# Graph network with layer norm on one core: the inverse deviations of the first four row blocks by Newton steps on GpSimd, and their early normalization

## The chip, the cores and the metric

One core of one Trainium2 chip runs the whole kernel. The metric is device time in microseconds (us). The kernel before has a median of 664.06 us over 3 runs (664.0 to 664.29).

## The reference, cut to what matters

The inputs are a node matrix x (2048 x 256) and an adjacency matrix adj (2048 x 2048, int32). Five steps of a gated graph network change a state that begins as x. Then an output head, a residual and a layer norm follow; the change is in that last part.

```python
state = x
for _ in range(5):
    a = concat([A @ (state @ in_W.T + in_b), A.T @ (state @ out_W.T + out_b), state])
    r = sigmoid(a @ r_W.T + r_b); z = sigmoid(a @ z_W.T + z_b)
    h_hat = tanh(concat([a_in, a_out, r * state]) @ h_W.T + h_b)
    state = (1 - z) * state + z * h_hat
hid = tanh(state @ o1_W.T + o1_b)
v = x + hid @ o2_W.T + o2_b
out = (v - mean(v)) / sqrt(var(v) + 1e-5)      # over the 256 columns of each row
```

## The kernel before, in words

Each engine has one instruction stream, written out by hand in program order, and semaphores order the streams among each other. An engine never passes a waiting instruction of its own, so the order of the source is the order of the work. (`general_path`, for a matrix that isn't symmetric, doesn't run here.)

The 2048 rows are 16 blocks of 128 rows (NB = 16), and 4 blocks make a chunk (BC = 4, NC = 4). The network's steps hold the state transposed (`stateT`, 128 partitions x 2 halves x 2048 columns), and every product is made of three matmuls of high and low parts: an operand is copied to its high part by ACT (`high`, L811) and its low part is a subtraction on DVE (`low`, L1136). The steps fill the span up to about 638 us. The change is in what follows them.

The stages at the end, for each chunk c:

- `update_last` (DVE, L1582): the last change of the state of chunk 3, six operations on 128x512 values at L1588, L1591, L1593 and L1595, behind the last gate at L1280.
- `final_split` (ACT `final_high`, DVE `low`): the high and low parts of the final state.
- `hidden` (TensorE, then ACT L1001 `hidden_tanh` and L1007 `hidden_high`): the hidden layer, its tanh and its high part. `split_hidden` (DVE, L1542) makes the low part. One of the eight low parts, half 1 of chunk 2, is made on GpSimd at L534.
- `output` (TensorE, L763): 24 matmuls of 256 columns; after each two blocks it signals `o_done`.
- `residual`, `moments`, `aggregated` (DVE, L1548 to L1566): adds x to two blocks (tile `a` of the profile, `y` in the code), takes the statistics of each block, and folds them to mean and variance (`mv`).
- `deviation` (ACT, L1109): sqrt(var + eps) for a batch of blocks. `inverse` (DVE, L1568): the reciprocal `rstd`, and `shift` = -mean * rstd.
- `normalize`: on ACT (L1115, a scaled Identity with the shift as bias), on DVE (L1578) for the blocks in `BY_DVE` = 12, 14, 15, and on GpSimd (L537) for `BY_POOL` = 2, 5, 10.
- The stores (SyncE, L454): blocks 0 to 3, 4 to 7, 8 to 11, 12 to 13, 14 to 15, in this order; each waits for the counts of blocks that ACT, DVE and GpSimd have normalized.

ACT's table of functions is changed once in this part: sqrt comes after the last tanh (the first sqrt, L1107, is there to make the load early). So the four deviation batches, (0 to 7), (8 to 11), (12, 13), (14, 15), all lie behind the last tanh, and chunk 0, whose variances are ready some 12 us earlier, waits with them. After the steps, GpSimd's stream holds only L534 and the three normalizations. Ahead of the last part DVE's stream (L1622 on) reads

```python
update_last(LAST, NC - 1)
final_split(3)
split_hidden(2)
residual(1, 0)
moments(1, 0)
```

and goes on with chunks 1 to 3 and the four `inverse` batches between them. ACT's stream there is: both `hidden_tanh(2, e)`; `final_high(3, e)` and `hidden_high(2, e)` in turn; `hidden(3)`; the table's load; the deviations and normalizations.

Of the kernel before, what the change touches and what calls it, by code (L numbers as in the profile page):

```python
# [11 lines left out]

# [1 line left out]

# [5 lines left out]
I32 = mybir.dt.int32  # L22
# [3 lines left out]
ALU = mybir.AluOpType  # L26
ACT = mybir.ActivationFunctionType

P = 128
CW = 512  # L30
EPS = 1e-5
# [10 lines left out]
def fast_path(nc, block, flag, flag_ready, y_stored, x, adj, in_W, in_b, out_W, out_b, r_W, r_b, z_W, z_b, h_W, h_b,  # L42
              o1_W, o1_b, o2_W, o2_b, out):
    N, D = x.shape
    NB, NC, DB = N // P, N // CW, D // P
    BC = CW // P
# [49 lines left out]
    with ExitStack() as ctx:  # L96
        def sb(name, shape, dt=F32):
            return ctx.enter_context(nc.sbuf_tensor(name, shape, dt))

        def sem(name):  # L100
            return ctx.enter_context(nc.semaphore(name))
# [31 lines left out]
        std = sb("std", [P, NB])  # L133
        rstd = sb("rstd", [P, NB])
        shift = sb("shift", [P, NB])
        above = sb("above", [P, NC * NP])
        differ = sb("differ", [P, 2 * NC])
        odd = sb("odd", [P, 3])
# [154 lines left out]
        hid_hi = sem("f_hid_hi")  # L293
        hid_lo = sem("f_hid_lo")
        hid_lo_pool = sem("f_hid_lo_pool")
        o_read_pool = sem("f_o_read_pool")
        o_done = sem("f_o_done")
        o_read = sem("f_o_read")
        xr_loaded = sem("f_xr_loaded")
# [33 lines left out]
        x_v = x.rearrange("(b p) d -> p b d", p=P)  # L333
        adj_v = adj.rearrange("(j p) i -> p j i", p=P)

        BATCHES = [(0, NB - 2 * BC), (NB - 2 * BC, NB - BC), (NB - BC, NB - 2), (NB - 2, NB)]
        BY_DVE = [NB - 4, NB - 2, NB - 1]
        BY_POOL = [2, 5, 10]

        starts = [c * BC for c in range(NC)] + [NB - 2, NB]  # L340

# [121 lines left out]
        def _(pool):  # L463
# [64 lines left out]
            pool.wait_ge(row_lo, row_count(1, (NC - 1, 1)))  # L528
            sum_blocks(1, range(6))

            c, e = 2, 1
            pool.wait_ge(fin_lo, NC * DB)
            pool.wait_ge(hid_hi, c * DB + e + 1)
            nc.gpsimd.tensor_tensor(hid_c[c % 2][LO][:, e, :], stateT[:, e, c * CW:(c + 1) * CW],  # L534
                                    hid_c[c % 2][HI][:, e, :].bitcast(F32), ALU.subtract).then_inc(hid_lo_pool, 1)

            for m in BY_POOL:  # L537

                pool.wait_ge(shift_ready, 1 + (m >= BATCHES[0][1]))
                nc.gpsimd.tensor_scalar(y[:, m, :], y[:, m, :], mv[:, m, 0:1], rstd[:, m:m + 1],  # L540
                                        ALU.subtract, ALU.mult).then_inc(y_pool, 1)

        @block.tensor
# [264 lines left out]
        def _(act):  # L809
# [197 lines left out]
            def hidden_high(c, e):  # L1007

                act.wait_ge(hid_act, c * DB + e + 1)

                wait(act, o_done, (c - 1) * (BC // 2))
                high(hid_c[c % 2][HI][:, e, :], stateT[:, e, c * CW:(c + 1) * CW], hid_hi)

            def hidden(c):

                for e in range(DB):
                    hidden_tanh(c, e)
                for e in range(DB):
                    hidden_high(c, e)
# [82 lines left out]
            for e in range(DB):  # L1102
                final_high(3, e)
                hidden_high(2, e)
            hidden(3)

            nc.scalar.activation(std[:, 0:1], ones[:, 0:1], ACT.Sqrt).then_inc(std_first, 1)  # L1107
            act.wait_ge(std_first, 1)
            def deviation(n):  # L1109

# [10 lines left out]
                                             bias=shift[:, m:m + 1]).then_inc(y_act, 1)  # L1121

            deviation(0)
            normalize(0, 0, BC + 1)
            deviation(1)
            normalize(0, BC + 1, 2 * BC)
            deviation(2)
            normalize(1, 2 * BC, 3 * BC)
            deviation(3)
            normalize(2, 3 * BC, 3 * BC + 2)  # L1130

        @block.vector
        def _(dve):
# [433 lines left out]
            def inverse(n):  # L1568

                a, b = BATCHES[n]  # L1570
                dve.wait_ge(std_ready, n + 1)
                nc.vector.reciprocal(rstd[:, a:b], std[:, a:b]).then_inc(rstd_ready, 1)
                dve.wait_ge(rstd_ready, n + 1)
                if n < len(BATCHES) - 1:
                    nc.vector.scalar_tensor_tensor(out=shift[:, a:b], in0=mv[:, a:b, 0], scalar=-1.0, in1=rstd[:, a:b],
                                                   op0=ALU.mult, op1=ALU.mult).then_inc(shift_ready, 1)

            def normalize(m):  # L1578
                nc.vector.tensor_scalar(y[:, m, :], y[:, m, :], mv[:, m, 0:1], rstd[:, m:m + 1],
# [59 lines left out]
            moments(3, 1)  # L1639
            inverse(2)  # L1640
            aggregated(3, 2, BC)
            normalize(BY_DVE[0])
            inverse(3)
            normalize(BY_DVE[1])
            normalize(BY_DVE[2])

    return len(starts) - 1

# [393 lines left out]
```

## Time and profile before

| what | value |
|---|---|
| median of 3 runs | 664.06 us |
| time of the profiled execution | 664.53 us |
| its span | 662.7 us |
| TensorE busy | 650.3 us, 98% |
| VectorE busy | 516.4 us, 78% |
| ScalarE busy | 348.5 us, 53% |
| GpSimd busy | 51.9 us, 8% |

The span is what the profiler records of the profiled execution; the 1.8 us by which its time is longer lie around it. PE is TensorE's matmul side, DVE VectorE, ACT ScalarE, POOL GpSimd, SP SyncE with its queue of DMAs. A line of the timeline gives start and duration in us, the engine, the source line, the operation, the tile written and the tiles read, the shapes and the count of instructions that were merged; a square bracket gives the idle time of the engine before it and who ended it. Two instructions of one engine that follow each other overlap a little, so the start-to-start distance is less than the duration.

### The profile page before, as it was taken

How to read it: one execution, taken by the hardware profiler on the slowest of the kernel's cores; microseconds unless marked ns; L12 is line 12 of the kernel's file. 1: busy time of each engine (PE TensorE's matmuls, PEld its weight loads, DVE VectorE, ACT ScalarE, POOL GpSimd, SP SyncE). 2: the span in 40 equal slices, each digit the busy share in tenths (PEclk: the TensorE clock that was granted, in tenths of full speed). 3: DMA queues.
4: the chain of work that ended last, by engine and by line, in shares of the span. 5: the costliest groups of instructions: out<-in, count | busy, mean ns of one | idle time of the engine just before them, and what ended most of it. 6: DMA issues, size and time to landing. Idle time of an engine off the chain costs nothing.

```text
span 662.7 us, 8577 instructions
## 1 busy us (share of the span) xinstructions
PE 650.3 (98%) x2940; PEld 539.6 (81%) x2940; DVE 516.4 (78%) x838; ACT 348.5 (53%) x486; POOL 51.9 (8%) x49
## 2 busy tenths in 40 slices
PE   8999999999999999999999999999999999999993
PEld 7888888888888888888888888888888888888883
DVE  4976878699687969967796997687789858855886
ACT  2873735477156337724562683366057525724646
POOL 0074034200500000000000000000000000000002
PEclk9999999999999999999999999999999999999998
DMA  8996533213000130300003022000322200013003
GB/s 293 305 405 242 169 130 107 42 42 54 2 0 32 50 47 33 50 14 0 32 33 62 0 63 32 0 32 32 52 44 60 35 1 1 0 64 127 1 2 130
DMA packets 90515, 46.72 MB, mean 70 GB/s; under 512 B 72176, under 2 KB 78960, under 8 KB 90224
## 3 DMA queue, kind: packets, MB, share of 16 engines
q1 hardware_dynamic: 86128, 45.77, 23.9%
q10 hardware_dynamic: 4352, 0.53, 0.5%
q8 instruction: 17, 0.28, 0.2%
q14 instruction: 18, 0.15, 0.1%
HBM read 32.12 MB, written 11.53 MB: 66 GB/s over the span
## 4 chain that ended last, share of the span: by engine, by line
PE 93%; DVE 2%; SPq 2%; DMA 2%; ACT 1%; issue 0%; DVEq 0%
PE bank L561 26%; PE bank L548 17%; PE bank L550 17%; PE bank L549 17%; PE bank L612 15%; DMA stage<-in_adj_dram 2%; SPq L393 1%; DVE stats L1560 1%; DVE a L1553 0%; DVE ring L1136 0%; SPq L389 0%; ACT a L1120 0%; DVE work L1593 0%; SPq L391 0%; DVE work L1588 0%
## 5 line engine op out<-in xcount | busy, mean ns | idle before, releaser
L561 PE MATMUL bank<-ring,rows 128*128 128x512 f32 x768 | 178.8, 389 | 0.3 <-ACT stateT L1091 0.3
L561 PEld LDWEIGHTS bank<-ring,rows 128*128 128x128 f32 x768 | 144.0, 188 | 30.6 <-ACT stateT L1091 0.5
L901 ACT ACTIVATE work<-work,bias 128x512 f32<-128x512 f32 x120 | 86.2, 723 | 155.5 <-DVE work L1280 154.9
L1280 DVE SCALAR_TENSOR_TENSOR work<-degree,deg_w,bank 128x512 f32<-128x512 uint16 x120 | 88.7, 745 | 57.5 <-PE bank L550 56.5
L548 PE MATMUL bank<-u_c,fold 128*128 128x512 f32 x240 | 93.5, 389 | 0.0
L550 PE MATMUL bank<-u_c,fold 128*128 128x512 f32 x240 | 93.4, 389 | 0.0
L549 PE MATMUL bank<-u_c,fold 128*128 128x512 f32 x240 | 93.4, 389 | 0.0
L612 PE MATMUL bank<-ring,rows 128*128 128x512 f32 x256 | 65.1, 391 | 0.0
L548 PE MATMUL bank<-st_c,own 128*128 128x512 f32 x160 | 62.3, 389 | 0.0
L550 PE MATMUL bank<-st_c,own 128*128 128x512 f32 x160 | 62.2, 389 | 0.0
L549 PE MATMUL bank<-st_c,own 128*128 128x512 f32 x160 | 62.2, 389 | 0.0
L833 ACT ACTIVATE ring<-sums,minus 128x1024 fp32r<-128x1024 uint8 x48 | 54.9, 1143 | 11.9 <-PE bank L612 11.3
L612 PEld LDWEIGHTS bank<-ring,rows 128*128 128x128 f32 x256 | 47.6, 188 | 11.1 <-issue 0.9
L550 PEld LDWEIGHTS bank<-u_c,fold 128*128 128x128 f32 x240 | 45.1, 188 | 9.4
L548 PEld LDWEIGHTS bank<-u_c,fold 128*128 128x128 f32 x240 | 45.0, 188 | 9.3
L549 PEld LDWEIGHTS bank<-u_c,fold 128*128 128x128 f32 x240 | 45.0, 188 | 9.3
L811 ACT ACTIVATE ring<-a 128x1024 fp32r<-128x1024 uint8 (+1 forms) x51 | 51.0, 1046 | 0.0
L1147 DVE CAST ring<-a 128x1024 fp32r<-128x1024 uint8 x64 | 44.5, 712 | 3.2 <-PE bank L561 2.9
L612 PE MATMUL bank<-ring,t_flat 128*128 128x512 f32 x192 | 46.7, 392 | 0.0
L612 PEld LDWEIGHTS bank<-ring,t_flat 128*128 128x128 f32 x192 | 35.4, 188 | 8.6 <-issue 0.6
L811 ACT ACTIVATE u_c<-bank 128x512 fp32r<-128x512 f32 x16 | 9.4, 591 | 60.6 <-PE bank L561 60.6
L534 POOL TENSOR_TENSOR ring<-stateT,ring 128x512 fp32r<-128x512 f32 x1 | 1.7, 1681 | 467.1 <-DVE rows L1136 467.1
(148 smaller groups left out, 985.0 us busy)
## 6 DMA issues: line engine op xcount, KB each, us to landing
stage<-in_adj_dram SPq DMA_DIRECT2D x15, 512.0 KB, 8.8
sums<-in_adj_dram SPq DMA_DIRECT2D x13, 512.0 KB, 8.5
turned_dram<-work SPq DMA_DIRECT2D x12, 512.0 KB, 2.6
rows<-turned_dram SPq DMA_DIRECT2D x192, 32.0 KB, 2.0
work<-in_x_dram SPq DMA_DIRECT2D x4, 512.0 KB, 10.2
x_dram<-work SPq DMA_DIRECT2D x4, 512.0 KB, 8.9
a<-x_dram SPq DMA_DIRECT2D x4, 512.0 KB, 5.3
a<-in_adj_dram SPq DMA_DIRECT2D x3, 512.0 KB, 11.5
```

Of the source, the lines that this page charges most:

```text
L393: sp.dma_start(x_raw[:, c * BC:(c + 1) * BC, :], x_v[:, c * BC:(c + 1) * BC, :]).then_inc(x_loaded[c], 16)
L548: nc.tensor.matmul(out_, wh, vh, start=first, stop=False)
L549: nc.tensor.matmul(out_, wh, vl, start=False, stop=False)
L550: return nc.tensor.matmul(out_, wl, vh, start=False, stop=last)
L561: m = nc.tensor.matmul(u_bank[2 * (c % 2) + d][:, :], rows[:, part, j, d * P:(d + 1) * P], tile[:, jj, :], start=(first and jj == 0 and pa ...
L612: last = nc.tensor.matmul(u_bank[BANK[kind]][:, :], product_rows(kind, part, 2 * p + jj), tile[:, jj, :], start=(kind in (P1, P5, P6, P4, ...
L811: nc.scalar.activation(out_, in_, ACT.Copy).then_inc(s, 1)
L833: nc.scalar.activation(ring[:, n % RING].rearrange("p j w -> p (j w)"), sums[:, 1 - side, m, h * 2 * CW:(h + 1) * 2 * CW], ACT.Identity, b ...
L901: nc.scalar.activation(gates[:, g, e, :], gates[:, g, e, :], ACT.Tanh if g == H else ACT.Sigmoid, bias=bias[:, g, e:e + 1]).then_inc(gate_ ...
L1147: nc.vector.tensor_copy(ring[:, n % RING], a8[:, 2 * side + kind, 2 * p:2 * p + 2, :]).then_inc(std_cast, 1)
L1280: nc.vector.scalar_tensor_tensor(out=gates[:, g, e, :], in0=degree[:, c * CW:(c + 1) * CW], scalar=deg_w[:, g, e:e + 1], in1=g_bank[s % 3] ...
L1560: nc.vector.bn_stats(stats[:, n, :], y[:, n, :]).then_inc(stats_ready, 1)
```

## The change

Sixteen small instructions on GpSimd, each waiting for the one before through a semaphore (`newton`), compute `rstd` and `shift` of blocks 0 to 3 from `mv`: var + eps, a first guess by integer arithmetic on its bits, three Newton steps of four instructions each, and the product with the mean, negated. GpSimd then normalizes block 3, and only after it comes its low part at L534. ACT waits for the result after `hidden_high(2, 1)` and normalizes blocks 0, 1 and 2 there, ahead of `hidden(3)`. The store of blocks 0 to 3 keeps its place in the SyncE queue. The batches of ACT and DVE become (4 to 7), (8 to 11), (12, 13), (14, 15). DVE normalizes block 15 alone; blocks 12 and 14 go to ACT, and DVE computes a shift for the last batch too.

```diff
--- before.py
+++ after.py
@@ -12,6 +12,7 @@
 
 
 
+import itertools
 from contextlib import ExitStack
 
 import concourse.bass as bass
@@ -133,6 +134,8 @@
         std = sb("std", [P, NB])
         rstd = sb("rstd", [P, NB])
         shift = sb("shift", [P, NB])
+        spread = sb("spread", [P, BC])
+        guess = sb("guess", [P, BC])
         above = sb("above", [P, NC * NP])
         differ = sb("differ", [P, 2 * NC])
         odd = sb("odd", [P, 3])
@@ -293,7 +296,8 @@
         hid_hi = sem("f_hid_hi")
         hid_lo = sem("f_hid_lo")
         hid_lo_pool = sem("f_hid_lo_pool")
-        o_read_pool = sem("f_o_read_pool")
+        newton = sem("f_newton")
+        early_ready = sem("f_early_ready")
         o_done = sem("f_o_done")
         o_read = sem("f_o_read")
         xr_loaded = sem("f_xr_loaded")
@@ -333,9 +337,9 @@
         x_v = x.rearrange("(b p) d -> p b d", p=P)
         adj_v = adj.rearrange("(j p) i -> p j i", p=P)
 
-        BATCHES = [(0, NB - 2 * BC), (NB - 2 * BC, NB - BC), (NB - BC, NB - 2), (NB - 2, NB)]
-        BY_DVE = [NB - 4, NB - 2, NB - 1]
-        BY_POOL = [2, 5, 10]
+        BATCHES = [(BC, 2 * BC), (2 * BC, 3 * BC), (3 * BC, NB - 2), (NB - 2, NB)]
+        BY_DVE = [NB - 1]
+        BY_POOL = [BC - 1, BC + 1, 2 * BC + 2]
 
         starts = [c * BC for c in range(NC)] + [NB - 2, NB]
 
@@ -528,17 +532,51 @@
             pool.wait_ge(row_lo, row_count(1, (NC - 1, 1)))
             sum_blocks(1, range(6))
 
+            links = itertools.count(1)
+
+            def link(instruction):
+
+                n = next(links)
+                instruction.then_inc(newton, 1)
+                pool.wait_ge(newton, n)
+
+            def scaled(out_, in_, factor, added):
+                link(nc.gpsimd.tensor_scalar(out_, in_, factor, added, ALU.mult, ALU.add))
+
+            def times(out_, a, b):
+                link(nc.gpsimd.tensor_tensor(out_, a, b, ALU.mult))
+
+            pool.wait_ge(aggr_ready, BC)
+            root, half_way = rstd[:, 0:BC], shift[:, 0:BC]
+            scaled(spread[:, :], mv[:, 0:BC, 1], 1.0, EPS)
+            scaled(root.bitcast(I32), spread[:, :].bitcast(I32), -0.5, 1597463007.0)
+            for _ in range(3):
+                times(half_way, root, root)
+                times(guess[:, :], half_way, spread[:, :])
+                scaled(half_way, guess[:, :], -0.5, 1.5)
+                times(root, root, half_way)
+            times(half_way, mv[:, 0:BC, 0], root)
+            nc.gpsimd.tensor_scalar(half_way, half_way, -1.0, 0.0, ALU.mult, ALU.add).then_inc(early_ready, 1)
+
+            def normalized(m):
+
+                if m < BC:
+                    pool.wait_ge(early_ready, 1)
+                else:
+                    pool.wait_ge(shift_ready, 1 + (m >= BATCHES[0][1]))
+                nc.gpsimd.tensor_scalar(y[:, m, :], y[:, m, :], mv[:, m, 0:1], rstd[:, m:m + 1],
+                                        ALU.subtract, ALU.mult).then_inc(y_pool, 1)
+
+            normalized(BY_POOL[0])
+
             c, e = 2, 1
             pool.wait_ge(fin_lo, NC * DB)
             pool.wait_ge(hid_hi, c * DB + e + 1)
             nc.gpsimd.tensor_tensor(hid_c[c % 2][LO][:, e, :], stateT[:, e, c * CW:(c + 1) * CW],
                                     hid_c[c % 2][HI][:, e, :].bitcast(F32), ALU.subtract).then_inc(hid_lo_pool, 1)
 
-            for m in BY_POOL:
-
-                pool.wait_ge(shift_ready, 1 + (m >= BATCHES[0][1]))
-                nc.gpsimd.tensor_scalar(y[:, m, :], y[:, m, :], mv[:, m, 0:1], rstd[:, m:m + 1],
-                                        ALU.subtract, ALU.mult).then_inc(y_pool, 1)
+            for m in BY_POOL[1:]:
+                normalized(m)
 
 
         @block.tensor
@@ -1102,9 +1140,13 @@
             for e in range(DB):
                 final_high(3, e)
                 hidden_high(2, e)
+            act.wait_ge(early_ready, 1)
+            for m in range(BC - 1):
+                nc.scalar.activation(y[:, m, :], y[:, m, :], ACT.Identity, scale=rstd[:, m:m + 1],
+                                     bias=shift[:, m:m + 1]).then_inc(y_act, 1)
             hidden(3)
 
-            nc.scalar.activation(std[:, 0:1], ones[:, 0:1], ACT.Sqrt).then_inc(std_first, 1)
+            nc.scalar.activation(std[:, BC:BC + 1], ones[:, 0:1], ACT.Sqrt).then_inc(std_first, 1)
             act.wait_ge(std_first, 1)
             def deviation(n):
 
@@ -1121,13 +1163,15 @@
                                              bias=shift[:, m:m + 1]).then_inc(y_act, 1)
 
             deviation(0)
-            normalize(0, 0, BC + 1)
+            normalize(0, BC, 2 * BC)
             deviation(1)
-            normalize(0, BC + 1, 2 * BC)
+            normalize(1, 2 * BC, 2 * BC + 1)
             deviation(2)
-            normalize(1, 2 * BC, 3 * BC)
+            normalize(1, 2 * BC + 1, 3 * BC)
+            normalize(2, 3 * BC, 3 * BC + 1)
             deviation(3)
-            normalize(2, 3 * BC, 3 * BC + 2)
+            normalize(2, 3 * BC + 1, 3 * BC + 2)
+            normalize(3, 3 * BC + 2, NB)
 
 
         @block.vector
@@ -1571,9 +1615,8 @@
                 dve.wait_ge(std_ready, n + 1)
                 nc.vector.reciprocal(rstd[:, a:b], std[:, a:b]).then_inc(rstd_ready, 1)
                 dve.wait_ge(rstd_ready, n + 1)
-                if n < len(BATCHES) - 1:
-                    nc.vector.scalar_tensor_tensor(out=shift[:, a:b], in0=mv[:, a:b, 0], scalar=-1.0, in1=rstd[:, a:b],
-                                                   op0=ALU.mult, op1=ALU.mult).then_inc(shift_ready, 1)
+                nc.vector.scalar_tensor_tensor(out=shift[:, a:b], in0=mv[:, a:b, 0], scalar=-1.0, in1=rstd[:, a:b],
+                                               op0=ALU.mult, op1=ALU.mult).then_inc(shift_ready, 1)
 
             def normalize(m):
                 nc.vector.tensor_scalar(y[:, m, :], y[:, m, :], mv[:, m, 0:1], rstd[:, m:m + 1],
@@ -1639,10 +1682,8 @@
             moments(3, 1)
             inverse(2)
             aggregated(3, 2, BC)
+            inverse(3)
             normalize(BY_DVE[0])
-            inverse(3)
-            normalize(BY_DVE[1])
-            normalize(BY_DVE[2])
 
     return len(starts) - 1
 
```

## Rows read from the trace of the kernel before

**Rows 1.** The page: busy time of each engine, its share of the span, instructions

```profile
PE 650.3 (98%) x2940; PEld 539.6 (81%) x2940; DVE 516.4 (78%) x838; ACT 348.5 (53%) x486; POOL 51.9 (8%) x49
```

**Rows 2.** The chain of work that ended last, from 637 us: start, duration, what

```profile
648.84 0.68 DVE ring L1136
...
655.01 1.47 ACT a L1120 x3
```

**Rows 3.** Timeline of ACT from 643 us

```profile
643.83 0.62 ACT L811 ACTIVATE ring<-stateT 128x512 fp32r<-128x512 f32 x1
646.31 1.37 ACT L1004 ACTIVATE stateT<-bank,bias 128x512 f32<-128x512 f32 x2 [1.86 <-PE bank L550]
647.57 1.14 ACT L811 ACTIVATE ring<-stateT 128x512 fp32r<-128x512 f32 x2
...
651.26 2.08 ACT L1120 ACTIVATE a<-a,shift,rstd 128x256 f32<-128x256 f32 x4 [0.69 <-DVE shift L1575]
...
656.50 0.30 ACT L1113 ACTIVATE std<-mv,eps 128x2 f32<-128x2 f32 x1
```

**Rows 4.** Timeline of DVE from 638 us

```profile
638.01 0.38 DVE L1566 BATCH_NORM_AGGREGATE mv<-stats 128x2 f32<-128x6 f32 x4
...
639.31 0.69 DVE L1588 TENSOR_TENSOR work<-work,stateT 128x512 f32<-128x512 f32 x1
...
644.57 0.69 DVE L1136 TENSOR_TENSOR ring<-stateT,ring 128x512 fp32r<-128x512 f32 x1
...
649.44 0.69 DVE L1553 TENSOR_TENSOR a<-bank,a 128x512 f32<-128x512 f32 x1
...
652.81 0.66 DVE L1553 TENSOR_TENSOR a<-bank,a 128x512 f32<-128x512 f32 x1
...
654.36 0.16 DVE L1575 SCALAR_TENSOR_TENSOR shift<-mv,rstd 128x4 f32<-128x4 f32 x1
...
656.14 0.16 DVE L1575 SCALAR_TENSOR_TENSOR shift<-mv,rstd 128x2 f32<-128x2 f32 x1
```

**Rows 5.** Groups of POOL's instructions, shapes apart: busy, mean ns, idle before

```profile
L477 POOL TENSOR_TENSOR deg_sum<-a 128x1024 uint32<-128x1024 uint32 x4 | 10.4, 2590 | 28.5 <-DVE a L1199 27.5 <-ACT t_flat L811 1.0
...
L540 POOL TENSOR_SCALAR a<-a,mv,rstd 128x256 f32<-128x256 f32 x3 | 3.7, 1224 | 5.8 <-DVE shift L1575 5.8
L477 POOL TENSOR_TENSOR deg_sum<-deg_sum 128x256 uint32<-128x256 uint32 x4 | 3.3, 824 | 0.3
...
L477 POOL TENSOR_TENSOR deg_sum<-deg_sum 128x128 uint32<-128x128 uint32 x4 | 1.8, 462 | 0.3
```

**Rows 6.** Timelines of DVE and POOL near 170 us and at 101 us

```profile
170.80 1.53 DVE L1147 CAST ring<-a 128x1024 fp32r<-128x1024 uint8 x1
...
101.93 1.04 POOL L507 TENSOR_TENSOR sums<-a,byte_two 128x512 uint32<-128x512 uint32 x1
...
170.29 1.49 POOL L507 TENSOR_TENSOR sums<-a,byte_two 128x512 uint32<-128x512 uint32 x1
```

**Rows 7.** Groups of DVE's instructions, shapes apart

```profile
L1147 DVE CAST ring<-a 128x1024 fp32r<-128x1024 uint8 x64 | 44.5, 712 | 3.2 <-PE bank L561 2.9 <-PE bank L612 0.2
```

**Rows 8.** Timelines of POOL and PE from 644 us

```profile
644.73 1.68 POOL L534 TENSOR_TENSOR ring<-stateT,ring 128x512 fp32r<-128x512 f32 x1 [467.09 <-DVE rows L1136]
...
646.79 0.28 PE L548 MATMUL bank<-t_flat,ring 128*128 128x256 f32 x1
...
652.43 0.28 PE L550 MATMUL bank<-t_flat,ring 128*128 128x256 f32 x1
```

**Rows 9.** Timeline of SP: the third and the fifth store's issue

```profile
656.56 0.37 SPq L460 DMA_DIRECT2D out_dram<-a  x1
...
657.85 0.71 SPq L460 DMA_DIRECT2D out_dram<-a  x1
```

**Rows 10.** Stretches of 1 us: length, busy of each engine, clock, DMA share, GB/s

```profile
658.00:659.00 1.00, 0.00 (x0) 0.00 (x0) 0.00 (x0) 0.00 (x0) 0.00 (x0) 0.50 1.03 345
...
661.00:662.00 1.00, 0.00 (x0) 0.00 (x0) 0.00 (x0) 0.00 (x0) 0.00 (x0) 0.50 0.06 23
```

## The prediction

> **What bounds the kernel now.** The page comes first: TensorE is busy for 98% of the span and GpSimd for 8% [rows 1]. That share says little here, since the change touches only what follows the network's steps, so the chain of waits is next. From 638.6 us on it runs almost only over DVE (the last state update, then chunk after chunk of low parts, residuals and statistics), and only at the end over ACT's last normalizations [rows 2]. The reader should see one place in it: at 648.84 DVE starts the second low part of hidden chunk 3, and ACT's high parts of the same chunk ended at 647.57 + 1.14 = 648.71 [rows 2, 3]. ACT has no slack there. If it is late with them, DVE is late by as much, and so is all that follows. In front of the last tanh, by contrast, ACT is idle for 1.86 us, until TensorE brings the hidden layer at 646.31 [rows 3]. That hole is where the change puts three normalizations. Last the stores: the fifth is issued at 657.85 [rows 9], and data flow at 345 GB/s in the stretch from 658 and still at 23 in that from 661 [rows 10].
>
> **Part 1, the Newton chain.** It can start when chunk 0 is aggregated, 638.01 + 0.38 = 638.4 [rows 4], and GpSimd is idle until 644.73 [rows 8]. The price of a 4-element instruction is in no row. The nearest are 2590 ns for 1024 elements and 462 for 128: slope 2.4 ns an element, so 0.17 us for 4 [rows 5]. The linked levels of the byte sums have 0.3 us of idle time over four, 0.08 each [rows 5]. So 0.25 us a step, and 16 steps make 4.0: ready at 642.4, while ACT asks for it at 643.83 + 0.62 = 644.45 [rows 3]. Undisturbed, the chain is free.
>
> But it isn't undisturbed. Near 170 us, where both engines read SBUF, a DVE cast takes 1.53 us instead of its mean of 0.71 [rows 6, 7], and the GpSimd instruction beside it 1.49 where the same form takes 1.04 at 101.93, beside a DVE instruction that reads PSUM [rows 6]. The two take turns, instruction by instruction: the cast issued at 170.80 ends only 0.55 us after GpSimd's, which began at 170.29 and ended at 171.78. L534 shows the same against a subtraction with two SBUF inputs: 1.68 us, beginning 0.16 us after it [rows 4, 8]. From 639.31 to 645.26 DVE runs nine such two-input instructions, almost gapless [rows 4]. In the 0.9 us ahead of 639.31 four steps fit. After that a step that has just ended starts the next one behind a DVE instruction that is already running, so it is one step per DVE instruction: nine more. Three are left at 645.26, 0.75 us. DVE pays too: each turn of GpSimd holds it for 0.17 less the 0.1 by which its own instructions overlap, 9 x 0.07 = 0.6. Ready at 645.26 + 0.75 + 0.6 = 646.6, 2.2 us after ACT asks. The ends: 0.12 us a step gives 645.9; no turns at all 642.4; a dearer tensor_scalar is a rival below. I take 646.6, because it's the cost that the nearest rows carry over to a small instruction.
>
> The Trainium skill says the same more strictly and against this change: in "SBUF — State Buffer", section "Who interferes with whom", a DVE instruction with two SBUF inputs contends with a GpSimd one that reads SBUF, and whoever issues second blocks fully. By that rule a step of 4 elements waits for a whole DVE instruction as a long one does, and the case below in which small steps slip through is excluded; no row here shows a step so small.
>
> **Part 2, ACT's three early blocks.** Four normalizations take 2.08 us with 0.59 for one [rows 3], so 0.5 from start to start, 1.5 for three. At the undisturbed time they would end by 646.05 in the hole of 1.86. At 646.6 the hole is over: the last tanh starts at 646.6 + 1.5 = 648.1, not at 646.31, **+1.8 us**. The high parts, the low parts on DVE and the rest of DVE's list shift by that; DVE's own 0.6 is inside it, since DVE would wait at the low parts anyway. The table's load and the deviations shift along.
>
> **Part 3, what queues on GpSimd and SyncE.** L534 now comes behind the chain and block 3 (1.22 us [rows 5]): 647.9, done at 649.2, where before it ended at 646.41 [rows 8]. `output(2)`, at 646.79 before [rows 8], starts then; `output(2)` and `output(3)` are 48 matmuls from 646.79 to 652.43 [rows 8], 0.12 apart, so 2.9 us each and 1.45 for two blocks. The first half is ready at 650.7, and DVE wants it at 649.44 + 1.8 = 651.2 [rows 4]: covered, by 0.5 us. Without that cover it would cost what exceeds it. `output(3)` then starts at 652.1, its first half is ready at 653.6 for a residual due at 652.81 + 1.8 = 654.6 [rows 4]. The store of chunk 0 goes out near 648; SyncE has nothing else queued then.
>
> **Part 4, the last three microseconds.** DVE loses blocks 12 and 14 and gains a shift (0.16, as [rows 4]). ACT loses blocks 0, 1 and 3 there and gains 12 and 14. Relative to the shifted time, ACT can start block 8 only after the shift at 654.36 [rows 4], about 0.2 after that starts, 654.57; the deviation of (12, 13) follows, then 9, 11 until 656.35, so the third store goes out at 656.44 instead of 656.56 [rows 9]. Block 12 starts at 656.35 behind the shift at 656.14 [rows 4], the last deviation at 656.85 instead of 656.50 [rows 3], the last shift near 657.4, block 14 until 658.2: the fifth store is issued at 658.3, 0.4 us later than now [rows 9]. It doesn't matter: from the third store on there is 1 MB to move, at 345 GB/s [rows 10] 3.0 us, and the third store's issue sets when that starts. That gives -0.1. And the thin flow of 661 to 662 us [rows 10], a fifteenth of the full rate, as one lagging DMA engine of 16 would leave behind 2 MB of stores in a row, may be gone once 0.5 MB leaves early: up to another -1.0. Ends -0.1 and -1.1; I take **-0.6**, halfway, since the lag's cause is in no row.
>
> **The sum.** +1.8 - 0.6 = +1.2 us on the profiled execution's own 664.53 (its span is 662.7), 665.7; that execution lies 0.5 above the median of the three runs, 664.06, so **665.3** for the median, +0.18%. A measurement of this kernel can tell about 0.2% from no change, 1.33 us: 662.7 to 665.4. The forecast is a small loss just inside that bound.
>
> **The rivals.**
>
> A. *Small steps slip through.* The chain ends at 642.4 as it would alone, but block 3 then takes its 1.22 us [rows 5] in the middle of the state update and holds DVE, about 1.1 us. The hidden layer of chunk 3 comes 1.0 late (TensorE waits for the low part). +1.0 - 0.6: 664.5. For it: 4 elements are little; against it: instructions of every size in the trace take turns.
>
> B. *Nothing collides at all.* The chain and block 3 run in idle time, ACT fills its hole, and only the end changes: -0.6, 663.5, at best -1.1, 662.9. This is as fast as the idea can be, since the path over DVE stays as long; it is still no difference that can be measured. Against it: the 1.53 us cast [rows 6].
>
> C. *Slower: GpSimd's tensor_scalar is dear to start.* Block-sized it takes 1.224 us for 256 elements where the two-input form takes 0.824 [rows 5]. If all 0.4 of that is start, a small one costs 0.57, and the chain has six. Two steps fit ahead of 639.31, nine are at DVE's turns, four of them long (4 x 0.5 + 5 x 0.07 = 2.3 of delay to DVE), five are left at about 0.45. Ready at 645.3 + 2.3 + 2.2 = 649.8, the tanh at 651.3, +5.0; the low parts can't hide it: 668.5 with the end's -0.6. It decides from about 0.25 us a tensor_scalar, where the forecast passes 0.2%; halfway to it stands 666.9. The Trainium skill speaks against C: "GPSIMD Engine Reference", section "4.1 Engine selection", has one-input operations roughly at line rate and two-input ones about twice as slow. By that the six would be the cheap ones of the chain; the rows with 256 elements show it the other way round.
>
> D. *The fifth store decides.* If the third store's data are through early, the 0.4 us by which the last shift is later stays: +1.8 + 0.4, 666.3. Against it: 3 us of transfer begin before.
>
> **How the numbers follow.** Forecast 0.47 (its own range 664.1 to 666.1: a chain that ends from 645.9 to 646.9, and the end's -0.1 to -1.1), A 0.17, B 0.12, C 0.14 with its halfway, D 0.05, the rest is what I don't see. Slower by over 0.2%: somewhat less than half of the forecast's case (0.21), C, D: 0.41. Faster by over 0.2%: only beyond B's best, 0.07. Within: 0.52. The range goes from 663.2, between B's value and its best, to 667.2, past C's halfway, and leaves out C's full price.
>
> **What would show it.** In the profile after: the sixteen POOL rows from 638.4 on, at 0.25 us until 639.3 and then at about 0.65, DVE's rate; at 0.25 throughout, A or B is right; at 0.5 and more ahead of 639.3, C. ACT's first early block at 646.7 with idle time before it that GpSimd ends; the last tanh at 648.1; DVE waiting at the low parts of chunk 3 for about 1.2 us. Two-input DVE rows of 0.75 in place of 0.69. No lag behind the last megabyte where -1.1 is right. The forecast is wrong if the last tanh starts before 647.3, or if DVE's wait lies elsewhere than at L1136.

## The result, and the profile after

The changed kernel takes 666.88 us (median of 20 runs, 665.36 to 668.18); the kernel before, on the same chip, takes 664.29 (20 runs, 663.29 to 665.99). The ratio is 1.0037, 95% interval 1.003 to 1.0043: 2.6 us lost, about twice the forecast's 1.2 and past the 0.2% that could be told from no change. The time lies inside the predicted range (663.2 to 667.2), and the direction is the forecast's. But the likeliest of the three outcomes was said to be "within 0.2%", and that one didn't come, and the range that the forecast gave its own mechanism, 664.1 to 666.1, was passed.

The profiled execution takes 666.98 us, its span is 665.2 against 662.7. One correction is needed for reading the two side by side: what lies ahead of the change is 0.69 us earlier in the trace after (chunk 0's aggregation at 637.32 instead of 638.01 [rows 4]), a difference that arises in the first 70 us, among the loads (at 67 us it is already 0.75), and that other executions have too, in other sizes. Where a time of after is compared with one of before, 0.69 is added first; such a sum is called a time "on the clock of before".

The page of the changed kernel, busy time by engine, says as little as it did before [rows 1]: GpSimd has 6 us more, TensorE 1.1.

```profile
PE 651.4 (98%) x2940; PEld 540.9 (81%) x2940; DVE 516.2 (78%) x837; ACT 349.5 (53%) x488; POOL 58.1 (9%) x65
```

The chain of work that ended last tells where to look. Before, it ran over DVE [rows 2]; now, from 637.8 us on, it runs over the sixteen GpSimd steps, block 3 and the low part behind it, and then, which nobody had forecast, over TensorE's matmuls of `output(2)`, 0.21 us each.

```profile
645.55 0.19 POOL shift L559
645.84 1.22 POOL a L567
647.07 1.24 POOL ring L575
648.30 0.14 issue
...
650.57 0.21 PE bank L588
...
653.15 0.70 DVE a L1597
```

GpSimd's timeline has the chain itself:

```profile
637.79 0.20 POOL L544 TENSOR_SCALAR spread<-mv 128x4 f32<-128x4 f32 x1 [459.80 <-DVE mv L1610]
...
638.35 0.20 POOL L547 TENSOR_TENSOR shift<-rstd 128x4 f32<-128x4 f32 x1
638.62 0.74 POOL L547 TENSOR_TENSOR guess<-shift,spread 128x4 f32<-128x4 f32 x1
...
643.30 0.71 POOL L547 TENSOR_TENSOR shift<-rstd 128x4 f32<-128x4 f32 x1
644.09 0.52 POOL L547 TENSOR_TENSOR guess<-shift,spread 128x4 f32<-128x4 f32 x1
644.70 0.19 POOL L544 TENSOR_SCALAR shift<-guess 128x4 f32<-128x4 f32 x1
...
645.55 0.19 POOL L559 TENSOR_SCALAR shift<-shift 128x4 f32<-128x4 f32 x1
```

Three steps take 0.20 us and start 0.28 apart. Nine take 0.52 to 0.74; these are the ones beside DVE's instructions with two inputs in SBUF. The last four are short again. Two lines of DVE's timeline show what decides:

```profile
639.34 0.69 DVE L1636 TENSOR_TENSOR work<-work 128x512 f32<-128x512 f32 x1
...
644.48 0.68 DVE L1597 TENSOR_TENSOR a<-bank,a 128x512 f32<-128x512 f32 x1
```

The step that starts at 639.45, inside the first of them, runs until 640.08, 0.05 us after DVE's instruction has ended at 640.03. So it is with all nine: whenever it started, each ends 0.05 to 0.06 us after the DVE instruction that was then running, so a long step is mostly waiting. Beside the second line, whose one input lies in PSUM (`bank`), the steps take 0.19 and 0.20 us.

The chain is ready at 645.74, 646.43 on the clock of before. Now ACT, the engine that waits for it:

```profile
645.77 1.58 ACT L1145 ACTIVATE a<-a,shift,rstd 128x256 f32<-128x256 f32 x3 [2.02 <-POOL shift L559]
647.26 1.24 ACT L1042 ACTIVATE stateT<-bank,bias 128x512 f32<-128x512 f32 x2
```

ACT stood 2.02 us for the chain, and the last tanh starts at 647.95 on the clock of before, 1.64 later than at 646.31 [rows 3]. What follows from that is in the list of waits from 637 us on (engine, what waited, for whom: total, times, longest):

```profile
PE bank L586 <- POOL ring L575: 2.2, 1, 2.2
ACT a L1145 <- POOL shift L559: 2.0, 1, 2.0
DVE ring L1180 <- ACT ring L849: 1.4, 1, 1.4
DVE a L1597 <- PE bank L588: 1.0, 2, 0.5
```

The third row is the forecast wait of DVE at the last low parts. The first and the fourth are the news: TensorE stands 2.2 us until the low part L575 comes, and after that DVE waits twice for `output(2)`, whose results the prediction had called covered. DVE's timeline gives the bill:

```profile
649.05 1.29 DVE L1180 TENSOR_TENSOR ring<-stateT,ring 128x512 fp32r<-128x512 f32 x2 [1.45 <-ACT ring L849]
650.89 0.69 DVE L1597 TENSOR_TENSOR a<-bank,a 128x512 f32<-128x512 f32 x1 [0.54 <-PE bank L588]
...
653.15 0.69 DVE L1597 TENSOR_TENSOR a<-bank,a 128x512 f32<-128x512 f32 x1 [0.50 <-PE bank L588]
...
654.82 0.66 DVE L1597 TENSOR_TENSOR a<-bank,a 128x512 f32<-128x512 f32 x1
```

The first residual starts 2.14 us later than before (650.89 + 0.69 against 649.44 [rows 4]), the third 2.70 (654.82 + 0.69 against 652.81 [rows 4]). So 1.5 us come from the late ACT and 1.2 from TensorE. The reason stands in the stretches of 1 us, in the same columns as [rows 10]:

```profile
647.00:648.00 1.00, 0.00 (x0) 0.00 (x0) 0.60 (x6) 1.00 (x3) 1.00 (x2) 1.00 0.00 0
648.00:649.00 1.00, 0.56 (x5) 0.59 (x6) 0.00 (x0) 1.00 (x3) 0.29 (x1) 1.00 0.63 214
649.00:650.00 1.00, 1.00 (x8) 1.00 (x7) 0.94 (x2) 0.98 (x3) 0.00 (x0) 0.55 0.93 310
650.00:651.00 1.00, 1.00 (x6) 1.00 (x6) 0.46 (x2) 0.99 (x2) 0.00 (x0) 0.50 0.00 0
```

At the end, first the third store's issue in SyncE's timeline:

```profile
658.42 0.37 SPq L464 DMA_DIRECT2D out_dram<-a  x1
```

From the third store's issue to the end of the span it is 665.2 - 658.42 = 6.8 us; before it was 662.7 - 656.56 = 6.1 [rows 9]. The group of the source line that issues all five (count, shortest, median and longest in ns, first and last start) and the stretch from 662 us show where: the last issue, from 660.3 on, takes 1716 ns, and 179 GB/s still flow in that stretch, where before the flow was already thin from 661 on [rows 10].

```profile
L464 SPq DMA_DIRECT2D out_dram<-a x5: 372/383/1716, 647.4 to 660.3; - x5
```

```profile
662.00:663.00 1.00, 0.00 (x0) 0.00 (x0) 0.00 (x0) 0.00 (x0) 0.00 (x0) 0.50 0.52 179
```

The account of the profiled execution: 1.5 (ACT late) + 1.2 (half clock) - 0.15 (third store nearer to DVE's list) + 0.65 (behind the third store) - 0.69 (earlier start) = 2.5, the difference of the spans.

### The profile page after: what moved, and what is told of

It is laid out like the page before. It is cut to its first block, busy times and chain, and to the rows that moved or that the text cites. A ratio compares the mean times of both kernels' runs of the same rounds, so it can differ in the third digit from the quotient of the medians.

```text
span 665.2 us, 8594 instructions
## 1 busy us (share of the span) xinstructions
PE 651.4 (98%) x2940; PEld 540.9 (81%) x2940; DVE 516.2 (78%) x837; ACT 349.5 (53%) x488; POOL 58.1 (9%) x65
## 4 chain that ended last, share of the span: by engine, by line
PE 95%; POOL 1%; DVE 1%; DMA 1%; ACT 1%; issue 0%; SPq 0%; DVEq 0%; POOLq 0%
PE bank L599 26%; PE bank L586 17%; PE bank L588 17%; PE bank L587 17%; PE bank L650 15%; PE bank L747 2%; DMA stateT<-in_L_gnn_in_W_dram 1%; PE bank L778 1%; PE bank L734 1%; ACT a L1162 0%; DVE stats L1604 0%; DVE a L1597 0%; POOL guess L547 0%; POOL shift L547 0%; POOL shift L544 0%
```

## The experiments

Each was run beside the kernel before on the same chip. "After" below is the changed kernel. Experiments 1 and 2 ask what the half clock costs, 3 and 6 what the late tanh costs, 4 and 5 what the end does, and 7 to 10 what the change is worth when nothing is late. In 3 and 7 to 9 there are two Newton steps instead of three. The texts of what was expected number the kernels otherwise: their e1 is experiment 1, e5 is 4, and e8, e9, e10 are 7, 8, 9.

**1. Block 3 behind the low part** (after, edited):

```
-            normalized(BY_POOL[0])
             c, e = 2, 1
             ...
             nc.gpsimd.tensor_tensor(hid_c[c % 2][LO]...).then_inc(hid_lo_pool, 1)
+            normalized(BY_POOL[0])
```

> The changed kernel, but GpSimd makes the low part of hidden chunk 2 (L575 of the changed kernel) ahead of normalizing block 3. Main theory (the low part comes late behind the chain and block 3, TensorE stands still for 2.2 us, its clock is halved and output(2) keeps DVE waiting twice): TensorE's pause shrinks to about 1.0 us, DVE no longer waits at the residuals of chunk 2, and the kernel is 1.2 us faster than the changed one, +1.4 over the kernel before. Rival 1 (only ACT's late blocks cost): no difference to the changed kernel, +2.6. Rival 2 (the end with its stores costs): +2.6 too, with TensorE's pause shorter all the same.

Measured: 666.01 us (665.42 to 666.38) against 663.98, ratio 1.0025, interval 1.0014 to 1.0037. Waits and two of the stretches of this kernel:

```profile
ACT a L1145 <- POOL shift L559: 2.0, 1, 2.0
DVE ring L1180 <- ACT ring L849: 1.4, 1, 1.4
...
PE bank L586 <- POOL ring L573: 0.9, 1, 0.9
```

```profile
647.00:648.00 1.00, 0.14 (x2) 0.17 (x2) 0.96 (x4) 1.00 (x3) 1.00 (x2) 1.00 0.00 0
...
649.00:650.00 1.00, 1.00 (x11) 1.00 (x10) 0.20 (x1) 1.00 (x3) 0.00 (x0) 1.00 0.09 32
```

ACT and DVE wait exactly as in after, TensorE stands for 0.9 us instead of 2.2, and the clock stays at 1.00, eleven matmuls a microsecond; all seven runs have 0.994 to 0.996. DVE's waits for `output(2)` are gone, and in the trace the third residual is 1.5 us late instead of 2.70. The kernel is now near the runs of after without the half clock (665.87). By the ratio it is 1.7 us slower than the kernel before (0.9 to 2.5), where +1.4 was expected; the interval just leaves out the rivals' +2.6, and it is the trace that speaks plainly.

**2. Ten matmuls in the pause** (after, with TensorE kept busy between `hidden(3)` and `output(2)` by products that nothing reads):

```
             hidden(3)
+            pe.wait_ge(o_read, BC // 2)
+            for _ in range(10):
+                nc.tensor.matmul(bank[2][:, :], o_w[:, HI, 0, 0, 0:P], fin_c[3][HI][:, 0, :], ...)
             output(2)
```

> The changed kernel, with ten further matmuls of 512 columns on TensorE between hidden(3) and output(2), into a bank that output(3) starts anew; they fill the pause. Their results are not used. Main theory: output(2) begins at the same time but at the full clock, 0.12 us a matmul instead of 0.21, DVE does not wait at L1597, and the kernel is about 1.2 us faster than the changed one, +1.4 over the kernel before. Rival (the pause itself costs and not the clock): the granted clock stays at 1.0 but DVE waits as before, +2.6.

Measured: 665.79 us (665.3 to 666.6) against 663.98, 1.0027 (1.0016 to 1.0038). Two stretches and the first residual of this kernel:

```profile
647.00:648.00 1.00, 1.00 (x7) 0.81 (x6) 0.90 (x6) 1.00 (x3) 1.00 (x2) 1.00 0.00 0
...
649.00:650.00 1.00, 1.00 (x10) 1.00 (x10) 0.65 (x2) 0.98 (x3) 0.00 (x0) 1.00 1.01 347
```

```profile
650.56 0.68 DVE L1600 TENSOR_TENSOR a<-bank,a 128x512 f32<-128x512 f32 x1
```

`output(2)` starts as late as in after (on the clock of before 649.15 and 649.13), TensorE is busy until then, no run has a clock below 0.995, and the residual has no idle time in front of it. So it was the standing still, not the late start of `output(2)`, that cost DVE its waits: a start at the same late time is covered when the matmuls run at full clock. By the ratio the kernel is 1.8 us slower than the one before (1.1 to 2.5), where +1.4 was expected. That is the evidence for the second term. It isn't evidence for a rule about how long a pause must be.

**3. Two Newton steps** (after, `range(3)` to `range(2)`; the roots are less exact):

> The changed kernel with two Newton steps instead of three (the reciprocal roots of chunk 0 are a little less exact): four instructions of the chain fewer. Main theory (the chain's end releases ACT, and behind DVE's two-input instructions a step takes 0.6 to 0.7 us instead of 0.28): the chain ends about 1.1 us earlier, the last tanh starts 1.1 us earlier, TensorE's pause is about 1.0 us; +0.4 to +1.4 over the kernel before. Rival (the three early blocks on ACT cost their 1.5 us wherever the chain ends): about +2.6, with the low parts of hidden chunk 3 as late as in the changed kernel.

Measured: 664.88 us (664.13 to 665.93), 1.0013 (1.0004 to 1.0022). Four links fewer, and ACT's and DVE's waits are 1.1 us shorter each:

```profile
PE bank L586 <- POOL ring L575: 1.1, 1, 1.1
ACT a L1145 <- POOL shift L559: 0.9, 1, 0.9
...
DVE ring L1180 <- ACT ring L849: 0.3, 1, 0.3
```

Of the 2.6 us, 1.7 are gone, but this edit changes two things: the chain ends 1.1 us earlier, and TensorE stands for 1.1 us only and no run has a clock below 0.995. The comparison at equal clock is that with experiments 1 and 2, at full clock and with the chain late, 1.7 and 1.8 us above the kernel before: here it is 0.9 (0.3 to 1.5). So a chain that ends 1.1 us earlier gives back about that, 0.8 to 0.9 us, though the intervals still overlap.

**4. The end alone** (the kernel before, with only the new assignment of blocks 12 and 14, the shifts and ACT's interleaving):

> The kernel before with the change's last part alone: DVE normalizes only block 15 and computes a shift for the last batch, ACT takes blocks 12 and 14 and starts block 8 ahead of the deviation of (12, 13). Nothing is early. Main theory: the compute of the last block ends 0.4 us later, and the stores hide it: 0 to +0.4 over the kernel before. Rival (the loss lies at the end): +1 or more.

Measured: 664.19 us (663.62 to 665.39) against 663.98, 1.0003 (0.9994 to 1.0012). The new assignment at the end is worth nothing that can be measured (-0.4 to +0.8). It is only one half of Part 4, though: that the end gets shorter because blocks 0 to 3 are stored early isn't in this kernel. Experiment 7 has both. DVE now waits 0.7 us for the last deviation on ACT, and in its profile the third store is issued 6.35 us ahead of the span's end (656.35 to 662.7) instead of 6.1.

**5. The fifth store issued by ACT** (the kernel before; asks whether SyncE's queue of issues holds the end):

```
-            for a, b in zip(starts, starts[1:]):
+            for a, b in zip(starts[:-1], starts[1:-1]):
             ...
+            act.wait_ge(y_dve, len(BY_DVE))
+            act.wait_ge(y_act, NB - len(BY_DVE) - len(BY_POOL))
+            act.dma_start(out_v[:, NB - 2:NB, :], y[:, NB - 2:NB, :]).then_inc(y_stored, 16)
```

> The kernel before with its fifth store issued by ACT instead of SyncE. If the store's issue is held by what the SyncE queue still has outstanding (0.71 us against 0.37 for the others, 1.72 in the changed kernel): its issue takes about 0.4 us and the data land up to 0.3 us earlier, -0.3 to 0. If the sixteen DMA engines themselves are the limit: no difference.

Measured: 664.16 us (663.59 to 664.62) against 664.11, 1.0002 (0.9993 to 1.0011). It changes nothing that can be measured; ACT's issue took 0.45 us, but in the same execution the fourth store's issue on SyncE, at 657.42, took 1.19. Which of these issues is stretched, and by what, stays open: a load of instructions by the queue q8 lies nearby in several of the traces, but not every issue beside one is long.

**6. The early blocks behind `hidden(3)`** (experiment 1, and ACT makes chunk 0's three blocks after the last tanh and its high parts):

```
-            act.wait_ge(early_ready, 1)
-            for m in range(BC - 1):
-                ...
             hidden(3)
+            act.wait_ge(early_ready, 1)
+            for m in range(BC - 1):
+                ...
```

> The changed kernel with two moves: GpSimd's low part ahead of block 3 (as in e1), and ACT's three early blocks behind hidden(3) instead of ahead of it, still before the table's load. Main theory (what costs is that ACT waits for the chain ahead of the last tanh): the last tanh and the low parts of hidden chunk 3 are on time, as in the kernel before; the 1.5 us of the three blocks now lie ahead of the table's load, so the first deviation comes 1.5 us late and DVE waits at its first reciprocal for about 1.2 us: +1.0 to +1.4 over the kernel before, 0.6 less than e1. Rival (DVE or TensorE suffers from GpSimd's chain itself): the low parts are late here too.

Measured: 665.25 us (664.82 to 665.89) against 664.11, 1.0017 (1.0009 to 1.0026). ACT's timeline and DVE's wait:

```profile
645.74 1.37 ACT L1042 ACTIVATE stateT<-bank,bias 128x512 f32<-128x512 f32 x2 [1.86 <-PE bank L588]
647.00 1.14 ACT L849 ACTIVATE ring<-stateT 128x512 fp32r<-128x512 f32 x2
648.05 1.57 ACT L1146 ACTIVATE a<-a,shift,rstd 128x256 f32<-128x256 f32 x3
```

```profile
DVE rstd L1616 <- ACT std L1155: 1.7, 2, 1.0
```

The tanh is on time (its idle time of 1.86 is that of [rows 3]), and DVE doesn't wait at the low parts any more. But the three blocks now push the table load and the first deviation, and DVE stands 1.0 us there. ACT has one hole, the one in front of the tanh; behind it the blocks cost again, only less.

**7. The chain on time** (after, with all that was late put right: two Newton steps, the low part ahead of block 3, and chunk 0 aggregated two gates earlier on DVE):

```
                         moments(0, h)
+                    aggregated(0, 0, BC)
                 gate(t, c, 4)
                 next_rows(4)
-                if last and c == NC - 1:
-                    aggregated(0, 0, BC)
```

> The changed kernel with all that makes the chain early: two Newton steps, chunk 0 aggregated ahead of the last two gates on DVE (0.64 us earlier), and GpSimd's low part ahead of block 3. Main theory: the chain ends at about the time when ACT asks for it, the last tanh starts at most 0.2 us after TensorE has brought its input, DVE waits nowhere at the low parts, and the kernel is as fast as the one with the end alone (e5): +0.2, within 0.3. So the early normalization is free here and gains nothing. Rival (the early store brings up to 1.0 at the end): -0.3 to -0.8.

Measured: 663.94 us (663.4 to 664.55) against 664.11, 0.9999 (0.999 to 1.0008). GpSimd's and ACT's timelines:

```profile
639.01 0.20 POOL L547 TENSOR_TENSOR rstd<-rstd,shift 128x4 f32<-128x4 f32 x1
639.29 0.56 POOL L547 TENSOR_TENSOR shift<-rstd 128x4 f32<-128x4 f32 x1
...
640.66 0.51 POOL L544 TENSOR_SCALAR shift<-guess 128x4 f32<-128x4 f32 x1
```

```profile
644.14 1.57 ACT L1145 ACTIVATE a<-a,shift,rstd 128x256 f32<-128x256 f32 x3
646.10 1.37 ACT L1042 ACTIVATE stateT<-bank,bias 128x512 f32<-128x512 f32 x2 [0.39 <-PE bank L588]
```

The blocks lie in the hole, without a wait in front of them, and TensorE still ends ACT's idle time, now 0.39. The same forms of instruction take 0.19 to 0.20 us ahead of DVE's work with two SBUF inputs and 0.51 to 0.65 beside it (the tensor_scalar was at 0.19 in after, above). The idea works as it was drawn, and the time is that of the kernel before: nearly rival B's picture, ACT's hole is filled and nobody waits for the chain, without a sign of B's 0.6 (the interval is -0.7 to +0.5).

**8. The same with the old end** (blocks 12 and 14 back on DVE):

> The kernel of e8, with blocks 12 and 14 given back to DVE as in the kernel before. Main theory: 0 within 0.3 against the kernel before, whatever the early blocks save on ACT, since DVE's list sets the end. Rival (ACT's freed time and the emptied store queue shorten the end): -0.4 or better, and this version beats both.

Measured: 663.74 us (663.27 to 666.37) against 664.11, ratio 1.0 (0.9991 to 1.0008). The medians lie 0.4 us apart, but the interval of the ratio (-0.6 to +0.5) has zero inside it. The main theory stands: with DVE's list as long as before, work taken from ACT in front of it buys nothing that shows.

**9 and 10. Less for DVE, with the early blocks and without.** In both, GpSimd also makes the second low part of hidden chunk 3, and the first reciprocal stands behind the second residual instead of ahead of it. In 9 the base is experiment 8, in 10 the kernel before.

```
+            c, e = 3, 1
+            pool.wait_ge(hid_lo_pool, 1)
+            pool.wait_ge(hid_hi, c * DB + e + 1)
+            nc.gpsimd.tensor_tensor(hid_c[c % 2][LO][:, e, :], ...).then_inc(hid_lo_pool, 1)
...
-            inverse(0)
             residual(2, 1)
+            inverse(0)
```

> The kernel of e9, with 0.6 us taken off DVE's list: GpSimd makes the second low part of hidden chunk 3 too (behind block 3, where it is idle), and DVE's first inverse stands behind the second residual of chunk 2, so that it doesn't wait for the deviation. Main theory (DVE's list sets the end, the early blocks don't): -0.4 to -0.7 against the kernel before, and no more than the next run gains without any early block. Rival (GpSimd's instruction and DVE's hold each other, or TensorE's output(3) comes late): 0 or slower.

> The kernel before with the same relief for DVE and nothing early. Main theory: -0.4 to -0.7 against the kernel before, the same as e10. Rival (only the early blocks make room for it on ACT): 0, with ACT's deviations and normalizations late.

Measured, against 664.27: with the early blocks 663.44 us (662.95 to 664.7), 0.9989 (0.998 to 0.9998); without 664.3 (663.82 to 664.85), 1.0 (0.9991 to 1.0009). My expectation that both would gain the same fell. The last part of ACT's timeline, first of 9, then of 10, and DVE's wait in 10:

```profile
654.07 1.08 ACT L1168 ACTIVATE a<-a,shift,rstd 128x256 f32<-128x256 f32 x2
655.31 0.30 ACT L1161 ACTIVATE std<-mv,eps 128x2 f32<-128x2 f32 x1 [0.17 <-DVE mv L1613]
```

```profile
654.45 1.57 ACT L1126 ACTIVATE a<-a,shift,rstd 128x256 f32<-128x256 f32 x3
655.92 0.28 ACT L1119 ACTIVATE std<-mv,eps 128x2 f32<-128x2 f32 x1
```

```profile
DVE rstd L1578 <- ACT std L1119: 0.2, 1, 0.2
```

In 9 ACT waits for DVE ahead of the last deviation; in 10 DVE waits for ACT, whose three blocks stand in front of it. That wait is 0.2 us and can't be the whole difference, since the last residual of 10 still starts 0.6 us earlier than before. More lies in the third store, which waits for ACT's blocks 8, 9 and 11. On the clock of before (0.44 added for 9, 0.14 for 10) it is issued at 655.66 in 9 and at 656.23 in 10, against 656.56 [rows 9]: 0.9 and 0.3 us earlier. In 9 ACT, free of chunk 0, has made block 8 ahead of the deviation of (12, 13); in 10 it is still at chunk 1 then. In both traces what lies behind the third store is 0.6 to 0.8 us longer than before, with a fifth issue of 1.57 and 1.28 us.

So the traces fit this reading: with DVE's list shortened ACT is the next bound, and only then do the three blocks that left it early count. It is argued from them and not shown by a run of its own, since 9 differs from 10 also in ACT's order at the end, which it has from the changed kernel. Version 9 is 0.8 us below the kernel before by the medians, 0.7 (0.1 to 1.3) by the ratio: the interval leaves out zero, narrowly, and the size is within the 0.2% that the chances went by.

## Why the prediction was right, and where its size failed

**The chain (Part 1): right to 0.2 us, partly by luck.** Ready at 646.43 against 646.6. Of its working, the step per DVE instruction held: three free steps instead of four, nine taking turns, four at the end instead of three. A free step costs 0.28 and not 0.25. The 0.6 us by which GpSimd's turns would hold DVE was wrong: DVE's nine instructions take 0.68 to 0.69 as before, and from 638.62 to 644.48 it is the same 5.86 us as from 639.31 to 645.17 in the trace of before. The missing 0.6 was for the most part made up by the dearer free steps and by the fourth step left at the end. That is the luck in it. On the rule of the Trainium skill in "SBUF — State Buffer", section "Who interferes with whom", that whoever issues second blocks fully (the page writes this out for DVE's two-port modes, and says of two SBUF inputs that they contend): the trace agrees for the steps of 4 elements (0.52 to 0.74 us beside DVE's instructions with two SBUF inputs, each ending just behind one of them, and 0.20 otherwise), and shows none of it in DVE's own durations.

**The last tanh (Part 2): right.** +1.64 us against +1.8, and +1.5 in DVE's list (1.5 in experiments 1 and 2 too). Experiment 3 moved the chain's end by 1.1 us, and the waits of ACT and DVE shrank by as much.

**The cover of `output(2)` (Part 3): the step that failed.** The prediction had the late start at 649.2 right (648.44 + 0.69 = 649.1) and called it "covered, by 0.5 us", with 0.12 us a matmul. The pause in front of it was never written down as a pause: TensorE, which in the trace of before doesn't pause once the loads are over, stands for 2.2 us, and soon after it runs at the half clock. From the start of `output(2)` to the first residual it is 2.45 us, not 1.45, since from the seventh matmul on they are 0.21 us apart, and what exceeds the cover is DVE's wait. The prediction had named its own sign of this: it is wrong "if DVE's wait lies elsewhere than at L1136". Of DVE's waits 1.4 us lie there (L1180 of after) and 1.0 us at the residuals. The missing term is +1.2 us, in 11 runs of 20. Experiments 1 and 2 take it away in two different ways, by a shorter pause and by work in it, and in both the clock stays up and the wait is gone. Without the half clock the cover held, as experiment 2 shows.

**The end (Part 4): -0.6 was mis-sized.** Experiment 4, the new assignment without the early store, has +0.2 with an interval from -0.4 to +0.8; experiment 7, with both, has -0.1 with -0.7 to +0.5, which just holds -0.6 and shows nothing of it. In after's trace what lies behind the third store is 0.65 us longer. Nor does any trace show a gain from the early store: from the third store's issue to the span's end it is 6.3 to 6.4 us with it (experiments 1, 3 and 7), 6.1 and 6.3 without (before, experiment 4). The lag behind the last megabyte does go in experiment 1 (316 GB/s in the stretch from 661, 10 from 662), but the span there still ends 6.4 us after the third store's issue. So whatever ends the program doesn't wait for that lag alone, and there is no sign that -1.1 was to be had. I had put the value halfway between two ends, of which one rested on a guess.

**The sum.** The chain's +1.5, the clock's +1.2 in eleven runs of 20, the end's 0 to +0.6 instead of -0.6. The direction and the first of two mechanisms were right, the second was missed, and the size was half. That the time lies inside the range is luck: the range went to 667.2 only to take in half of rival C, which didn't happen.

**The rivals.** A (small steps slip through) and B (nothing collides) fell on the nine long steps. C (a dear tensor_scalar) fell on its 0.19 us, the same as the two-input form; the measured time lies next to its halfway value of 666.9, but by another mechanism. The page "GPSIMD Engine Reference", section "4.1 Engine selection", of the Trainium skill, compares GpSimd with VectorE. For two inputs the trace agrees with its factor of about two (L575 1.26 us against 0.69 on DVE for 128x512, 1.8 times), for one input not with its line rate (a block normalized in 1.22 us against 0.38 on DVE, 3.2 times). At 4 elements the two forms cost the same, so the page's cheap one-input step isn't what made C fall. D (the fifth store) isn't settled. In after the last block is ready and the fifth store issued 0.4 us later than DVE's list alone would make them (+3.1 against +2.7), as D had it; but experiments 4 and 7, with a fifth store 0.5 and 0.4 us late, have intervals that hold both 0 and +0.4, and moving its issue to ACT in the kernel before changed nothing.

**What stays open.** Why the issue of one store takes 0.37 us in one execution and 1.72 in another. Why the 2.2 us pause brings the half clock in only 11 of 20 runs. Whether the new end costs or gains something below 0.3 us when the chain is on time, since the intervals of experiments 7 and 8 overlap. And how the 0.8 us of experiment 9 divide between the early blocks, ACT's order and the stores.

## What to carry to other kernels

Price a moved step by every engine that queues behind it: here the late low part, covered as long as the clock held, cost 1.2 us by letting TensorE stand, since the matmuls after the pause ran at half clock in more than half of the runs. A serial chain of tiny operations on GpSimd advances one step per DVE instruction while DVE works on two SBUF inputs, so start such a chain before that work or shorten it. And relieving an engine off the path may pay only together with a shorter path: the early blocks were worth nothing alone, and about 0.8 us (0.1 to 1.3) once DVE's list had been cut.

## What the runs showed that was not expected

- A pause of TensorE of 2.2 us between matmuls was followed by 3.4 us at half clock (matmul to matmul 0.21 instead of 0.12 us) in the trace, and by its mean clock in 11 of 20 runs; pauses of 0.9 to 1.1 us (experiments 1, 3 and 6) in none of three traces, and by the mean clocks in none of 29 runs. What decides between the two wasn't tried further.
- GpSimd's 4-element instructions, of one input or two, take 0.19 to 0.20 us and 0.28 with the semaphore link to the next. Beside DVE's instructions with two SBUF inputs they take 0.51 to 0.74, whatever is left of that instruction and 0.05 to 0.06 more, while DVE's stay at 0.68 to 0.69.
- The issue of the same store on SyncE took between 0.37 and 1.72 us.
